# A second attention whose score maxima are taken in two groups of eight heads per image

## What is computed

```python
qkv = src @ in_proj_w.T + in_proj_b              # 16 heads of width 16
scores = einsum('bhqd,bhkd->bhqk', q, k) / math.sqrt(dh)
attn = softmax(scores, axis=-1)
dense_output = ctx @ out_proj_w.T + out_proj_b   # ctx = attn @ v
QK = einsum('bqr,bkr->bqk', Q, K) / math.sqrt(R) # one more head, width 64
aw = softmax(QK, axis=-1)
topv, topi = top_k(aw, 51)                       # keep the 51 largest of a row
sparse_attn = topv scattered / (sum + 1e-09)
sparse_output = sparse_attn @ V
fused = sig * dense_output + (1 - sig) * sparse_output
```

## Time and profile before

| | us |
|---|---|
| median of 3 runs | 1481.87 (1479.94 to 1483.51) |
| profiled execution, device time | 1477.99 |
| its span, first to last instruction | 1476.2 |
| PE busy | 1118.4 (76% of the span) |
| DVE busy | 765.7 (52%) |
| ACT busy | 384.5 (26%) |
| POOL busy | 452.8 (31%) |
| mean granted TensorE clock | 0.832 of full |

### The profile page before, as it was taken

One profiled execution on the slowest core, in us unless ns is written; L12 is line 12 of the kernel. 1 busy time (PEld: TensorE's weight loads), 2 busy tenths in 40 slices (PEclk: granted clock), 3 DMA queues, 4 the chain that ended last, 5 costly groups with the idle time before them and its releaser, 6 DMA issues. The chain is left out here.

```text
span 1476.2 us, 21690 instructions
## 1 busy us (share of the span) xinstructions
PE 1118.4 (76%) x6799; PEld 807.9 (55%) x6799; DVE 765.7 (52%) x1788; ACT 384.5 (26%) x951; POOL 452.8 (31%) x527
## 2 busy tenths in 40 slices
PE   0358886750999990359999999999734999779888
PEld 0257774650677660235665665665422899646555
DVE  8955663230122224445556556656512377578885
ACT  0333331000222220114333334333210444222221
POOL 5941010117000007511202202211000577456665
PEclk9989998555899995667779769878657899989999
DMA  6016000102121113144314315414031200000000
GB/s 217 2 41 216 0 0 1 54 15 100 55 64 58 60 48 99 36 77 95 85 34 105 84 32 105 96 37 90 18 74 37 101 0 0 1 1 14 14 7 22
DMA packets 53403, 81.06 MB, mean 55 GB/s; under 512 B 8544, under 2 KB 45736, under 8 KB 52176
## 3 DMA queue, kind: packets, MB, share of 16 engines
q1 hardware_dynamic: 50128, 71.71, 19.1%
q0 software_dynamic: 3200, 8.43, 1.8%
HBM read 52.23 MB, written 27.62 MB: 54 GB/s over the span
## 5 line engine op out<-in xcount | busy, mean ns | idle before, releaser
L1933 DVE TENSOR_REDUCE fa_nm<-fa_ps 128x2 f32<-128x514 f32 x128 | 82.9, 690 | 74.4 <-PE fa_ps L2154 73.6
L1292 PE MATMUL ex_ps<-we_raw,ex_xT 128*128 x320 | 118.3, 494 | 0.0
L1773 ACT ACTIVATE fa_eT<-fa_ps 128x512 f32<-128x512 f32 x128 | 73.6, 590 | 81.7 <-PE fa_ps L2207 80.3
L1086 POOL DMA_INDIRECT ex_got<-y_rows,ex_pos_i x34 | 32.1, 943 | 196.9 <-DMA y_rows<-ex_y 186.8
L2945 PE MATMUL qf_ps<-qf_wg,qf_xT 128*128 128x352 f32 x272 | 89.9, 480 | 2.1 <-ACT qf_xT L2786 1.4
L2154 PE MATMUL fa_ps<-fa_ks,fa_qs 64*128 64x258 f32 x256 | 71.4, 408 | 15.4 <-DMA fa_ks<-fa_qk_rows 10.8
L447 PE MATMUL tk_ps<-tk_u,tk_qb 64*32 64x64 f32 x1024 | 22.8, 266 | 71.4 <-POOLq L314 59.7
L2207 PE MATMUL fa_ps<-fa_qs,fa_ks 66*128 66x256 f32 x256 | 71.3, 373 | 6.9 <-ACT fa_eT L1773 6.9
L1219 DVE COPY ex_hT<-ex_ps 128x384 f32<-128x384 f32 x40 | 22.3, 558 | 100.1 <-PE ex_ps L1301 100.1
L2154 PEld LDWEIGHTS fa_ps<-fa_ks,fa_qs 64*128 64x128 f32 x256 | 50.7, 258 | 40.6 <-issue 23.4
L2945 PEld LDWEIGHTS qf_ps<-qf_wg,qf_xT 128*128 128x128 f32 x272 | 50.6, 194 | 37.3 <-issue 6.6
(11 more groups left out here) (435 smaller groups left out, 2509.3 us busy)
## 6 DMA issues: line engine op xcount, KB each, us to landing
we_raw<-in_L_ffn_W SPq DMA_DIRECT2D x24, 384.0 KB
fa_qs<-fa_qk_rows SPq DMA_DIRECT2D x16, 514.0 KB
fa_ks<-fa_qk_rows SPq DMA_DIRECT2D x32, 257.0 KB, 9.9
x_rows<-tk_zero SPq DMA_DIRECT2D x1, 5120.0 KB, 19.1
ex_xin<-x_rows SPq DMA_DIRECT2D x40, 128.0 KB
y_rows<-ex_y SPq DMA_DIRECT2D x40, 128.0 KB, 1.7
fa_rsb<-fa_rs_rows SPq DMA_DIRECT2D x8, 528.0 KB
fa_qk_rows<-fa_qhl SPq DMA_DIRECT2D x32, 128.5 KB
```

Source lines behind the costliest of these rows:

```text
L1086: g.indirect_dma_start(out=got[0:n, a, t, :], out_offset=None, in_=y_rows[:, :], in_offset=bass.IndirectOffsetOnAxis(ap=pos_i[0:n, a, t:t ...
L1292: last = mm(ps[:, bank + t % 2, 0:HD], xT[:, t % 2, k, :], raw[:, ds(e, 1), m, k * HD:(k + 1) * HD], start=(k == 0), stop=(k == KC - 1))
L1773: cp(eT[:, j % 8, :], ps[:, ST + j % 2, :], ACT.Exp).then_inc(z["e_ready"], 1)
L1933: nc.vector.tensor_reduce(nm[:, :, j], ps[:, b:b + 2, 0:TOK], AX.X, ALU.max, negate=True).then_inc(z["max_done"], 1)
```

## The change

It rewrites the tables and orders of `fused_attention` on all engines. The number of products, maxima, rounds and DMAs stays the same.

- **Heads in two groups.** Heads 0 to 7 of image u+1 are scored in body u (slots 12 to 15, `EARLY_AT`). Heads 8 to 15 are scored in the next body, in slots 0 to 3 (`LATE_AT`), heads 8 and 9 ahead of the projections of the following image, which waits for their maxima since it uses the same banks. The prologue scores eight heads.
- **Selection later on DVE.** The 14 rounds stand in slots 4 to 11 (`ROUNDS_AT`), four of them ahead of `add_attention` and ten behind it. Before, ten stood ahead and four behind.
- **Values later.** `values` of u+1 go from slots 8 and 9 to 15 and 16, on all three engines.
- **End of PE's body.** Slot 17 now has the transposes of the maxima, the last quad, `turn_rows`, and `class_context` as the last piece. The first quad goes from slot 4 to 9, `turn_weights` from 13 to 12, with all eight early heads behind it.
- **SP, POOL.** `strips_in` of k stands behind `max_rows(u, 1)`, `max_rows(u+1, 0)` ahead of `sums_out`, `values_out` last. `low_maxima(u, 1)` stands behind `shared_context(u-1)`. `kblk` gets a second buffer, and one semaphore is split in two.

```diff
-    ROUNDS_AT = {0: 2, 2: 2, 3: 2, 4: 2, 5: 2, 6: 1, 7: 2, 8: 1}
-    HEADS_AT = {10: (0, 1), 11: (2, 3), 12: (4, 5), 13: (6, 7), 14: (8, 9), 15: (10, 11), 16: (12, 13), 17: (14, 15)}
+    ROUNDS_AT = {4: 2, 5: 2, 6: 1, 7: 2, 8: 2, 9: 2, 10: 2, 11: 1}
+    LATE_AT = {0: (8, 9), 1: (10, 11), 2: (12, 13), 3: (14, 15)}
+    EARLY_AT = {12: (0, 1), 13: (2, 3), 14: (4, 5), 15: (6, 7)}
...
                 for sl in range(SLOTS):
-                    if sl == 1 and more:
+                    for j in LATE_AT.get(sl, ()):
+                        head_max(u, j)
+                    if sl == 0 and more:
                         high_parts(u + 1, 1 - p)
+                    if sl == 3:
+                        high_maxima(u, 1)
                     if sl == 6 and not first:
                         add_attention(u - 1)
-                    if sl == 7 and not first:
                         statistics(u - 1)
-                    if sl == 8 and more:
+                    if sl == 7 and more:
                         class_max(u + 1)
-                    if sl in (8, 9) and more:
-                        values(u + 1, 1 - p, sl - 8)
                     if more:
-                        for j in MAXES_AT.get(sl, ()):
+                        for j in EARLY_AT.get(sl, ()):
                             head_max(u + 1, j)
...
+                    if sl == 15 and more:
+                        high_maxima(u + 1, 0)
+                        values(u + 1, 1 - p, 0)
+                    if sl == 16 and more:
+                        sparse_max(u + 1)
+                        values(u + 1, 1 - p, 1)
...
             def projected(u, j, name):
                 pe.wait_ge(z["x_taken"], u + 1)
                 if not isinstance(u, int) or u:
-                    pe.wait_ge(z["max_done"], N * u + j - 1)
+                    pe.wait_ge(z["max_done"], N * (u - 1) + 9 + j)
...
             def body(u, p, first, more, two):
                 for sl in range(SLOTS):
-                    for j in TURNED_AT.get(sl, ()):
-                        turned_scores(u, p, j)
+                    for j in LATE_AT.get(sl, ()):
+                        head_scores(u, p, j, more)
                     if sl == 0 and more:
                         projected(u + 1, 0, "q_ps")
                         projected(u + 1, 1, "k_ps")
...
+                    if sl in (9, 13):
+                        quad(u, p, {9: 0, 13: 2}[sl])
+                    if sl in TURNED_AT:
+                        turned_scores(u, p, TURNED_AT[sl])
+                    if sl == 4 and more:
+                        sparse_operands(u + 1)
+                    if sl == 5 and not first:
+                        project(u - 1, 1 - p, more=more)
+                    if sl == 6:
+                        turn_maxima(u, 1, first)
+                    if sl == 7 and more:
+                        class_query(u + 1)
+                    if sl == 8:
                         class_keys(u, p)
...
+                    if sl == 12:
                         turn_weights(u, more)
-                    if sl == 15:
+                    if sl == 14:
+                        turn_class_weights(u)
+                    if sl == 15 and more:
+                        values(u + 1, 0)
+                    if more:
+                        for j in EARLY_AT.get(sl, ()):
+                            head_scores(u + 1, 1 - p, j)
+                    if sl == 16 and more:
+                        sparse_scores(u + 1)
+                        values(u + 1, 1)
+                    if sl == 17:
+                        if more:
+                            turn_maxima(u + 1, 0, False)
+                        quad(u, p, 3)
+                        if two:
+                            turn_rows(u + 2)
                         class_context(u, p)
```

More of the change, by code:

```diff
@@ L1545, in body @@
                     sparse_class_values(u + 1, 1 - p)
-                    values_out(u + 1, 1 - p)
+                    max_rows(u + 1, 1 - p, 0)
                 sums_out(u, p)
                 sums_in(u)
-                if more:
-                    max_rows(u + 1, 1 - p, 0)
                 shares_out(u)
                 shares_in(u)
+                if more:
+                    values_out(u + 1, 1 - p)
             for dst, src in loads:
@@ L2107, in sparse_operands @@
             def sparse_operands(u):
-                pe.wait_ge(z["q_taken"], KC * (u + 1))
+                if isinstance(u, int) and u == 0:
+                    pe.wait_ge(z["q_taken"], KC)
+                else:
+                    pe.wait_ge(z["max_done"], N * (u - 1) + 15)
                 for j in range(2):
@@ L2255, in turn_class_weights, with project @@
                 last.then_inc(z["wc_ps"], 1)
-            def project(u, p, done=False):
+            def project(u, p, done=False, more=False):
                 pe.wait_ge(z["cn_ready"], u + 1)
@@ L2281, in body @@
                         projected(u + 1, 1, "k_ps")
-                    if sl == 1:
-                        turn_maxima(u, 1, more)
-                    if sl == 2:
-                        class_keys(u, p)
-                    if sl == 3 and more:
-                        sparse_operands(u + 1)
-                    if sl in (4, 7, 10, 14):
-                        quad(u, p, {4: 0, 7: 1, 10: 2, 14: 3}[sl])
-                    if sl == 5 and not first:
-                        project(u - 1, 1 - p)
@@ L2305, in body @@
-                    if more:
-                        for j in HEADS_AT.get(sl, ()):
-                            head_scores(u + 1, 1 - p, j)
-                            if j == 9:
-                                sparse_scores(u + 1)
-                    if sl == 17 and two:
-                        turn_rows(u + 2)
+                    if sl in (9, 13):
+                        quad(u, p, {9: 0, 13: 2}[sl])
+                    if sl in TURNED_AT:
+                        turned_scores(u, p, TURNED_AT[sl])
@@ new lines, in body @@
+                    if sl == 4 and more:
[7 more added lines that the diff above has]
+                    if sl == 8:
+                        class_keys(u, p)
+                    if sl == 10:
+                        if more:
+                            turn_class_probs(u + 1)
+                        quad(u, p, 1)
@@ L2333, in _ @@
             turn_class_probs(0)
[L2334 removed]
+            for j in range(8):
                 head_scores(0, 0, j)
[L2336 to L2338 removed]
+            sparse_scores(0)
+            turn_maxima(0, 0, True)
             turn_rows(1)
```

157 lines of the change are left out of this document (69 added, 88 removed).

## The result

The changed kernel takes 1602.8 us (median of 4 runs, 1594.7 to 1608.5), where the kernel before takes 1480.9 in runs on the same chip. The ratio is 1.0812 [1.0779, 1.0844]: slower by 8%. The prediction was 1585 us, slower, range 1515 to 1622. The profiled execution takes 1600.35 us with a span of 1598.6, at a mean granted clock of 0.813 (0.832 before).

What follows compares the result with a forecast made beforehand. PE was taken to bound the kernel, at two clocks; the change uncovers the sums' reduction and DVE's selection. 6 x 14.3 + 6 + 11 = +103 us on 1477.99 gives 1581, plus 3.9 is 1585; range 1515 to 1622, own range 1555 to 1612.

Steps and rivals of the forecast that it cites:

- 1: PE idle ahead of q: Start of an image: q's projection waits for a late maximum queued behind the softmax sums' reciprocals; PE idles some 3.7 us.
- 2: split of k done: After the projections, 5.4 us, to 10.4, the split of k ends 1.4 us later, at 11.8.
- 3: last late maximum: Six late maxima on DVE, 4.1 to 4.7 us, with the split of the maxima to 16.4.
- 4: four rounds done: Four selection rounds on DVE at 1.2 us each, 4.8 us, to 21.2.
- 5: output projection: Previous image's output projection on PE waits for the sums' second leg until 17.9, takes 7.6 us, ends at 25.5.
- 6: `turn_weights`: Addition, statistics, `class_max`, ten rounds and POOL's scaling take 19.1 us; `turn_weights` starts at 44.6, PE idling about 10 us.
- 7: slots 12 to 17: PE's work from `turn_weights` to `class_context`: 24 us taken, between about 15 at full clock and 27.2 from low-clock rows.
- image 0, image 7: First and last images, reckoned apart: image 0 +6 us (-3 to +9), image 7 +11 us (+2 to +12).
- Clock back: Rival: full clock returns in slots 12 to 17, which take 17 to 18 us; +51, time 1533; chance 0.18.
- PE the bound and faster: Rival: heads mixed with dense products hold PE's clock up; about 10 us less an image, 1420 in all; chance 0.07.
- Partly covered: Rival: the waits are as told but partly covered; an image at 56 to 58, in all 1495 to 1510; chance 0.07.
- Two colder stretches: Rival: output projection starts cold and slots 12 to 17 never warm; 74.9 us an image, +145, 1627; chance 0.12.

## Why the prediction was right, step by step

It named the sign, the place and the two mechanisms, and came out 18 us (1.1%) low, within its own range of 1555 to 1612. Both waits stand in the trace with the releasers that it named, and the terms below fit one by one, so the sum is not right by errors that cancel: they all point the same way. Of its signs one missed: the issues of `sums_out` are 70.0 to 72.5 us apart, not 65 to 70. For the image shown above, predicted and measured:

| step | predicted | measured |
|---|---|---|
| 1: PE idle ahead of q | 3.7 us | 3.82 |
| 2: split of k done | 11.8 | 12.4 |
| 3: last late maximum | 16.4, split with it | 16.3, split held to 18.5 |
| 4: four rounds done | 21.2 | 23.2 |
| 5: output projection | 17.9 to 25.5 | 18.5 to 25.6 |
| 6: `turn_weights` | 44.6, PE idle about 10 | 45.0, idle 9.37 |
| 7: slots 12 to 17 | 24 us | 25.7 |
| image | 68.6 | 70.6 (mean 71.1) |
| image 0, image 7 | +6, +11 | +7.7, +11.7 |

The steps that were mis-sized:

- *Step 5, in two images of six.* The output projection starts at t = 21.5 and 21.8 there. In them PE came to 0.50 again among the late heads, behind the projection of q and k, and `sparse_operands` (L2108), 1.95 us above, takes 3.69. I had taken this start as set by the sums alone. In these two `turn_weights` starts at 47.8 and 48.0, in the other four at 44.6 to 45.5. The mean is 45.9, 1.3 above my 44.6, and 1.0 of this is theirs.
- *Step 7.* I took 24 between 15 and 27.2; the mean is 25.2. The clock did come back as the rival said, but only with the values: 0.74 and 0.82 there. The kernels with 72 half-row products and with two kinds of product show that head scores alone do not bring it back from 0.50; for quads and the class context no run shows it apart.
- *Step 3.* The split of the maxima took 2.1 us instead of 0.17. It cost nothing here, since step 5 ended later anyway; in the kernel with seven rounds and four dense products it did.
- What lies behind the last `sums_out` I held at nothing; it took 2.5 us more.

- *The wait ahead of the addition* was put at 4 us and is that on the average.

6 x (1.3 + 1.2) + 1.7 + 0.7 + 2.5 = 19.9, for the 19.4 by which the sum (103) was short of 122.4.

Three slips of the working move nothing: the terms shown for the sums' second leg add up to 17.7, not 17.9, those of step 6 to 19.2, not 19.1, and without the wait for the output projection the chain gives 40.3, not 40.4.

**The rivals.** *Clock back* (1533) was true in a small part: slots 12 to 17 took 25.2 us, where it had 17 to 18 and a stretch all at 0.50 has 27.2 by my sum. *PE the bound and faster* is out: the chain reached `turn_weights` at 45, as against the 39.3 that it needed. I had held that no order with the selection behind the late heads could get there; the kernel with seven rounds ahead of the addition does, at 39.2, and still takes 64.9 us an image, since slots 12 to 17 stay at 25.8. The kernel that reaches it at 38 to 42, with the idle times used, had no clock to gain either. *Partly covered* is out, with both waits at their full length. *Two colder stretches* is out for the output projection, which ran at 1.00 in the six middle images and partly cold (0.68) only in image 7.

**The rule weighed.** The rows had PE 5.00 of 5 us busy at 0.50, and the run with two kinds of product has 10.40 of 10.40 us busy at 0.50. The Trainium skill, page "TensorE: Matmul & The Clock Gate", section "What's actually happening", ties the full clock to sustained busy time alone; by that the 48 products would have come to the full clock, and they did in none of four bodies. The measurement decides: here two kinds of product that keep PE equally busy came out differently, and what in them decides is open (see the run). Its other section, "HAM oscillation — how this bites in real kernels", agrees: behind 9.37 us of idle time the clock was 0.50.

## What to carry to other kernels

Before a long chain is moved behind a boundary, list what lies beside it now; a reduction that took 17.5 us from end to end was free beside six heads, projections and turned scores, and cost 8.4 us an image with the six heads gone from beside it. An idle time is to be priced with the clock of what stands behind it: moving a part of it from ahead of one dense piece to directly ahead of the next took 2.2 us of idle time an image away and added 5.2 of busy time. Products that keep a full clock may be unable to bring it back. Whether the kernel's own dense work would pay directly behind an idle time that can't be removed was not tried.

## What the runs showed of the hardware

- **Keeping and regaining the clock are two things.** 72 products of 64 rows by 258 columns (float32r) took 9.01 us where they began at 1.00 (six bodies) and 15.85 where they began at 0.50 (one), without changing level in either. 48 of them from 0.50 took 10.69 us in each of four bodies. Twelve products of 128 rows by 512 columns (float32) from the same state reached 1.00 within the row, three times of three, and so did the projection of q and k, 128 rows by 257 columns, six times of six in the kernel before.
- **Some DVE operations are held by a POOL product.** The split of the maxima, a TENSOR_SCALAR of 16 elements, takes 0.17 us, but where it starts during POOL's product of 128x1028 it ends with it: 944.81 + 2.11 against 944.52 + 2.37, and likewise in 5 of 7 bodies (1.30 to 2.11 us). It is not new with the change. In the kernel before the same product, at 726.18 for 2.38 us, holds the COPY of three columns in the selection, 0.17 us elsewhere. DVE waits 1.66 us ahead of the next addition all the same:

```profile
727.00 1.59 DVE L1954 COPY fa_rep<-fa_top 128x3 f32<-128x3 f32 x1
```

It is not a matter of short operations either. In the kernel with `class_context` last a SCALAR_TENSOR_TENSOR of 128x257, 0.43 us elsewhere, takes 2.21 us and ends with the product (857.31 + 2.21 against 856.88 + 2.36). MAX8 and MATCH_REPLACE8 beside the same product kept their 0.43 and 0.42 us in the kernel with seven rounds, where the split came some 0.5 us ahead of the product each time. The Trainium skill, page "GPSIMD Engine Reference", section "1. Specifications", names contention at the shared SBUF interfaces with DVE instructions that run in a 2-port mode or have two SBUF inputs. The SCALAR_TENSOR_TENSOR, with two inputs, agrees, with the number above; whether the split and the COPY ran in a 2-port mode no run here shows.
